# Adjacent partitions instead of every third for the stacked rows of q and k

## What is computed

```python
q = split(x @ W_q.T)
k = split(x @ W_k.T)
v = split(x @ W_v.T)
attn = jax.nn.softmax(scale * jnp.einsum('bnqd,bnkd->bnqk', q, k), axis=-1)
o = jnp.einsum('bnqk,bnkd->bnqd', attn, v)
```

## Time and profile before

| | us |
|---|---|
| median of 3 runs | 1066.43 |
| lowest, highest | 1065.25, 1072.98 |
| the profiled execution, its own time | 1072.98 |
| its span in the profile | 1071.2 |
| TensorE busy in the span | 1004.5 (94%) |
| VectorE, ScalarE, GpSimd busy | 759.0, 537.0, 271.8 |
| mean share of the 16 DMA engines, queue of SP and queue of ScalarE | 20.4%, 6.9% |

### The profile page before, as it was taken

The page is one execution under the profiler, slowest core; times in us unless marked ns, Lnnn a source line. Parts: engine busy times, 40 slices in busy tenths (PEclk is TensorE's granted clock), DMA queues, the critical chain, the costliest instruction groups (busy, mean ns, idle before and its releaser), DMA issues.

```text
span 1071.2 us, 17062 instructions
## 1 busy us (share of the span) xinstructions
PE 1004.5 (94%) x5380; PEld 619.5 (58%) x5380; DVE 759.0 (71%) x1208; ACT 537.0 (50%) x1119; POOL 271.8 (25%) x260
## 2 busy tenths in 40 slices
PE   5999999996999899999989999998999899999868
PEld 4777777774434455545645564565556456645656
DVE  5888788995667786777577767867776776785232
ACT  4466455443555555446355535644564564456221
POOL 1265422220000321222122213212221321122133
PEclk9999999996999899979989998999999899999879
DMA  9545574442321220313024031302221230310000
GB/s 285 136 103 131 139 163 113 109 104 60 109 61 42 69 66 2 79 50 64 13 67 106 8 78 51 65 11 69 71 43 45 66 65 3 80 36 1 25 0 21
DMA packets 93685, 75.11 MB, mean 70 GB/s; under 512 B 44848, under 2 KB 79736, under 8 KB 93632
## 3 DMA queue, kind: packets, MB, share of 16 engines
q1 hardware_dynamic: 79040, 57.20, 20.4%
q10 hardware_dynamic: 14592, 17.25, 6.9%
HBM read 27.73 MB, written 12.61 MB: 38 GB/s over the span
## 4 chain that ended last, share of the span: by engine, by line
PE 81%; DVE 10%; issue 4%; DMA 2%; SPq 1%; ACT 1%; POOL 0%; DVEq 0%; POOLq 0%; ACTq 0%
PE bank L1091 19%; PE bank L358 13%; PE bank L923 11%; PE bank L942 10%; PE bank L1135 9%; PE raw_pair L882 5%; PE bank L808 5%; DVE rowmax L890 3%; PE bank L1003 3%; PE bank L381 2%; DVE amax L440 1%; PE bank L858 1%; PE bank L1059 1%; DVE x_in L1044 1%; SPq L912 1%
## 5 line engine op out<-in xcount | busy, mean ns | idle before, releaser
L890 DVE TENSOR_REDUCE rowmax<-raw_pair 128x2 f32<-128x1024 f32 x256 | 312.9, 1222 | 132.3 <-PE raw_pair L882 132.3
L931 ACT ACTIVATE probs<-bank 128x512 f32<-128x512 f32 x512 | 281.7, 596 | 231.3 <-PE bank L923 229.4
L923 PE MATMUL bank<-q_stack,k_stack 50*128 50x512 f32 x512 | 198.2, 458 | 2.4 <-DMA q_stack<-shift_rows 1.3
L358 PE MATMUL bank<-up_w,xs_part 128*128 128x512 f32 x768 | 193.8, 405 | 6.7 <-issue 5.3
L882 PE MATMUL raw_pair<-k_stack,q_stack 48*128 48x512 f32 x512 | 178.1, 472 | 21.9 <-DVE rowmax L890 21.3
L358 PEld LDWEIGHTS bank<-up_w,xs_part 128*128 128x128 f32 x768 | 143.7, 192 | 41.9 <-issue 8.5
L942 PE MATMUL bank<-probs,v_ext 128*17 128x512 f32 x1024 | 141.9, 627 | 0.3
L1121 POOL TENSOR_TENSOR hid<-scratch,hid 128x512 fp32r<-128x512 f32 x64 | 82.5, 1288 | 225.9 <-ACT hid L1117 225.9
L923 PEld LDWEIGHTS bank<-q_stack,k_stack 50*128 50x128 f32 x512 | 82.0, 191 | 88.1 <-issue 52.5
L1091 PE MATMUL bank<-xf_part,gate_w 128*128 128x512 f32 x384 | 108.0, 417 | 4.9 <-POOL xf_part L1081 4.2
L1091 PEld LDWEIGHTS bank<-xf_part,gate_w 128*128 128x128 f32 x384 | 68.8, 192 | 68.2 <-issue 51.5
(11 more groups left out here) (121 smaller groups left out, 1108.6 us busy)
## 6 DMA issues: line engine op xcount, KB each, us to landing
q_stack<-split SPq DMA_DIRECT2D x48, 128.0 KB, 2.9
q_stack<-hid SPq DMA_DIRECT2D x48, 128.0 KB, 2.9
xk<-xT SPq DMA_DIRECT2D x32, 128.0 KB, 2.9
xt<-x_tok SPq DMA_DIRECT2D x32, 128.0 KB, 2.7
x_spill<-x1t ACTq DMA_DIRECT2D x32, 128.0 KB, 2.5
xa_spill<-xa ACTq DMA_DIRECT2D x32, 128.0 KB, 2.3
x_in<-xa_spill SPq DMA_DIRECT2D x8, 512.0 KB, 4.9
k_stack<-split ACTq DMA_DIRECT2D x32, 128.0 KB, 4.8
```

Source lines behind the costliest of these rows:

```text
L358: last = nc.tensor.matmul(bank[j][:], xs_part[a][:, m % 2, k, :], up_w[w][:, k, col + j * W:col + (j + 1) * W], start=(i == 0), stop=(i == ...
L890: nc.vector.reduce_max(rowmax[:, e:e + RAWS + 1:RAWS], raw_pair[:], AX.X).then_inc(raw_read, 1)
L923: nc.tensor.matmul(score_bank[c % 3][:], k_stack[rows, slot, kt * P:(kt + 1) * P], q_stack[rows, slot, :], start=True, stop=True).then_inc ...
L931: nc.scalar.activation(probs[:, (kt % 2) * J + j, :], score_bank[c % 3][:], ACT.Exp).then_inc(exp_done, 1)
```

## The change

Two edits. In `stack_dma` the destination of copy r of a half is now the block of 16 adjacent partitions 64*half + 16*r to 64*half + 16*r + 15; before it was every third partition from 64*half + r on, over 46 partitions. Both stacks change in the same way, so that the sum of a matmul has the same 48 products in another order. In `stack_sp` the two loops are exchanged: SP issues the three copies of half 0 of q and then those of half 1, and before the halves alternated. The bytes, the number of DMAs, the sources, the waits and the semaphores stay.

```diff
@@ stack_dma
-            eng.dma_start((q_stack, k_stack)[w][64 * half + r:64 * half + ROWS:ROWS // HD, G * m:G * m + G, :]
+            eng.dma_start((q_stack, k_stack)[w][64 * half + HD * r:64 * half + HD * (r + 1), G * m:G * m + G, :]
                           .bitcast(f32), staging(m, w)[part][64 * half:64 * half + 64, :].bitcast(f32)) \
                 .then_inc(stacked[m], 16)
@@ stack_sp
-                for r in rows:
-                    for half in range(2):
+                for half in range(2):
+                    for r in rows:
                         stack_dma(sp, m, w, half, r)
```

## The result

| | us |
|---|---|
| median before, in the runs beside the changed kernel | 1066.39 |
| median after, of 4 runs | 1104.72 (1102.66 to 1105.38) |
| ratio, 95% interval | 1.0346, 1.0307 to 1.0383 |
| the profiled execution after, its span | 1102.93, 1101.1 |

The change costs 38.3 us, 3.5%, where 7.2 were forecast. The profiled execution of before was the slowest of its runs, so that the two profiled executions differ by 29.95 us only, and the two spans by 29.9. The granted clock goes with this: its mean is 0.952 in the profiled execution of before, while the 30 runs of that kernel that were timed beside the experiments have 0.957 to 0.963 where they took up to 1069.5 us, and 0.950 to 0.954 where they took more.

A forecast was written before the change was run, and what follows sets the result against it. TensorE, busy 94% of the span, was taken to bound the kernel. Set 1 landing 1.6 us later, less 0.4 of room and 0.3 absorbed, gave 0.9 us in 8 passes, 7.2: 1066.43 to 1074 us, range 1065 to 1092.

The forecast's parts named there:

- rival 5: Faster: copies and row maxima land earlier; all present waits for DMAs are worth 2.0 us; over 1% faster has chance 0.03.
- The exchanged loops: SP's q copies of one half, issued behind each other, land slower, by up to 0.8 us for such a DMA.
- The adjacent partitions: Set 1's last pair lands 5.2 us after issue instead of 3.6, 1.6 later, bounded from above by 5.5.
- Rival 3: Blocks of 16 partitions halve the rate of both sets to about 92 GB/s: 91 us more, 1157 us; chance 0.08.
- Rival 2: Both sets' streams get a third slower: 17 us more, 1083 us; chance 0.25, shared with a wait with longer low clock.
- What is absorbed: At set 1's raw matmul 0.3 us of delay are absorbed before VectorE's row maximum; after that nothing is.
- rival 4: A wait lengthens the low clock after set 1's reader: some us, 14 if 3.4 us more per pass; no separate chance.
- (a): TensorE's raw matmul or its weight load waits for a k_stack DMA, about 0.9 to 1.2 us, eight times.
- (c): The window of set 1 shows fewer GB/s than 183 over a longer time, and set 0 too.
- (d): The first reader of set 0 still doesn't wait, save perhaps in batch 0.
- (b): ScalarE's last pair of set 1 lands 5.2 us after its issue; above 6 means Rival 2 or Rival 3.
- (e): The low-clock stretch after half-step 6 keeps its length; if it grows, rival 4 adds to the time.

The follow-up runs named there:

- Runs 1: The changed kernel with the loops of before (halves alternate), so only the destination is changed: 1102.53 us, ratio 1.0332 to the kernel before.
- run 7: The changed kernel's adjacent partitions for only one set, the other as before: set 1 only 1097.18 us, ratio 1.0296; set 0 only 1072.14 us, ratio 1.0070.
- run 2: The kernel before, every third partition kept, with only the loops of stack_sp exchanged: 1072.22 us, ratio 1.0037.
- run 4: A separate kernel with nothing but such copies and a store of zeros; twelve with halves in turn: 0.65 us each at every third partition, 1.02 as blocks.
- runs 3: The kernel before with copies 0 and 1 on every second of the first 32 partitions and copy 2 in a block: 1068.23 us, ratio 1.0001.
- run 5: The copies-only kernel with streams of twelve blocks and pairs of queues: 1.18 us per copy into block 0; pairs' last landing 6.6 to 7.6 us after issue.

## Why the prediction was wrong

*What bounds the kernel, and the place of the loss*: right. Set 1 with 0.4 us of room, in eight passes; set 0 safe but for the one out of batch 0. Runs 1 and 7 show both. One reading was too wide: the 2.0 us of the earlier trace rows are the waits of the stacks' readers, and not all present waits for DMAs as rival 5 has it; TensorE also waits 5.2 us for the DMA of `qT` in phase 1, which the change doesn't touch.

*The exchanged loops*: right in size (run 2), and a small part of the whole.

*The adjacent partitions*: this is the step that failed, the term of the sum that was mis-sized. I bounded the last landing of set 1 from above by the slowest pair of the trace, 5.5 us, and took 5.2, 1.6 us later. It was 7.9, 4.3 later. The bound was none. With 4.3 in its place the same sum gives 8 x (4.3 - 0.7) + (4.3 - 1.5) = 31.6 us instead of 7.2, which is most of the 38.3. A crowded pair of the old form shows what a backlog does when each copy still moves at 167 GB/s, not what happens when each copy holds the engines half as long again. The right question was what one copy takes in a stream: 0.65 us spread and 1.02 as a block (run 4), so that for the eleven behind the first it is 11 x 0.37 = 4.1 us more, near the 4.3. This compares well because the kernel issues its twelve in 7.3 us, as run 4 does in 7.0. No row of before had the price of a block; that twelve copies of set 0 took 10.2 us where their issue took 6.8 showed only that they stood in each other's way already.

*The port rule of the Trainium skill*, which I gave only as a rival of 0.08 in its strictest form, says rightly which copies are slow (runs 3 to 5). By its two rates a copy takes 1.3 against 0.7 us, an estimate; the streams show 1.18 into one block, 1.02 into blocks by turns, and 0.65 spread, bound by the issue. Rival 3 took it as half of 183 GB/s with nothing overlapping, 92; measured were 115 to 121. Rival 2, a third slower, had 137 and 1083 us. The truth lies between them: 12.4 us for set 1 against 10.4 and 17.2. My argument against both, that two queues write different blocks at the same time, is refuted: they hardly overlap (run 4, two queues; run 5, pairs).

*What is absorbed*: 0.3 us were read off one pass. The waits of 3.3 us on average lengthened the six passes by 15.6 / 6 = 2.6 us, so that 0.7 us of each are absorbed. They take the place of waits for VectorE: in batch 5 the two raw matmuls of half-steps 6 and 7 wait 1.20 + 0.51 us for the maximum, before 1.34 and 2.23, and all such waits of raw matmuls fall from 21.3 to 13.9 us. The prediction had said that nothing is absorbed after the first 0.3 us; that was wrong, and made the loss smaller than the waits.

*The clock* (rival 4): I put it on the passes that have a thin stretch already. There it did little. It came in batch 0, where the sum had put it at nothing, which I had dismissed as a pass with fillers: 5.2 us after two waits, and in run 7 one wait of 3.7 us, whose kernel lost 5.9.

*The signs set in advance*: (a), (c) and (d) came as named, (a) three times as large; (b) said that above 6 us rival 2 or 3 holds, and it did. (e), the low stretch kept about its length in the six passes (29.0 and 30.8 us by the sum above), and grew in batch 0, where I had not looked.

*What the 38.3 us are made of.* Of the 29.9 us between the spans, waits for the copies are 30.2, the absorbed part takes off some 5, and the clock in batch 0 gives 5.2: 30 or so, which leaves no room for a large part of another kind. The other 8 us between the medians are that the profiled execution of before was 6.6 us above its median and that of after 1.8 below. Before's slower runs are those with the lower granted clock, as said above; in which stretch they lose it no trace shows, since only one of them was profiled.

## What to carry to other kernels

Price a DMA by what it takes in the stream in which it stands, not alone: 0.5 us more in landing became 4.3 us at the end of twelve. Give a copy into few partitions a step (2, 3 and 4 all did here), so that its 16 partitions are spread over more ports, and look for how far the last copy is from its reader: 0.4 us of room was all that hid the set. A high DMA share does not say by itself what the engines are doing: it was 1.02 at 116 GB/s for blocks, and 0.94 at 210 GB/s for spread copies on two queues (run 4, windows 34 to 45 and 170 to 176). Read it beside the rate; where the share is full and the rate is low, a slow copy lengthens those behind it on both queues.

## What the runs showed of the hardware that I had not expected

- Copies into blocks on different ports hardly overlap: blocks 0 and 16 in turn, or one half and the other, take 1.02 to 1.03 us per copy, 128 GB/s for eight ports, little better than 111 for four (runs 4 and 5). A second queue changes nothing for them: 14.3 against 14.5 us for twelve (run 4).
- Step 4 lands 128 KB in 2.2 us, step 2 in 2.4, step 3 in 2.5, blocks in 3.0 to 3.2, each alone. The step between step 2 and step 4, with two partitions per port in both, is not explained by the fullest port.
- A single wait of 3.7 us in a stretch of TensorE with little other idle time was followed by a fall to a mean granted clock of 0.72 over 30 us (run 7, set 0, one execution). How long the low clock lasts is not set by the length of the wait: after waits of 3.51 and 3.52 us in batch 0 of the changed kernel it lasted some 14 and 3 us, after the 3.72 of run 7 some 17, with TensorE busy nearly without a gap all the while.
